# Attention layers: probabilities times V moved behind the scores and transposes of its step; semaphores cleared by ranges

## The reference, cut to what matters

```
# layer 0 (16 heads of 32)
qkv = (xin @ Wqkv.T + qkv_bias) ...; q, k, v = (qkv[0], qkv[1], qkv[2])
qn = q / jnp.maximum(jnp.linalg.norm(q, axis=-1, keepdims=True), 1e-12) * sm
scores = jnp.einsum('bhqd,bhkd->bhqk', qn, kn) + attn_bias
p = jax.nn.softmax(scores, axis=-1)
o = jnp.einsum('bhqk,bhkd->bhqd', p, v)
return o @ Wproj.T + bproj
# layer 1: 16 query heads of 32 on 4 key heads, rotary embedding, a mask that leaves
#          a window of 64 keys, every 64th key and no later block of 128
# layer 2: 8 query heads of 64 on 1 key head, rotary embedding, no mask
# each: scores -> softmax -> times V -> output projection -> added to x
```

## Time and profile before

| | us |
|---|---|
| runs, median (lowest to highest of 3) | 2793.87 (2792.99 to 2800.02) |
| the profiled execution's own time | 2805.94 |
| its span in the profile | 2804.2 |
| PE busy | 2407.7 (86%) |
| DVE busy | 1560.3 (56%) |
| ACT busy | 1279.6 (46%) |
| POOL busy | 902.2 (32%) |

### The profile page before, as it was taken

The page is one execution under the profiler, slowest core; times in us unless marked ns, Lnnn a source line. Parts: engine busy times, 40 slices in busy tenths (PEclk is TensorE's granted clock), DMA queues, the critical chain, the costliest instruction groups (busy, mean ns, idle before and its releaser), DMA issues. The chain is left out here.

```text
span 2804.2 us, 47282 instructions
## 1 busy us (share of the span) xinstructions
PE 2407.7 (86%) x15672; PEld 1952.3 (70%) x15672; DVE 1560.3 (56%) x4470; ACT 1279.6 (46%) x3188; POOL 902.2 (32%) x988
## 2 busy tenths in 40 slices
PE   6888888897699999588788768889899999996776
PEld 4777777786487888466565557777688888885565
DVE  5867767776553434565556466557543333334866
ACT  3666766767321111377665656566531111102443
POOL 0333343423476667123222213223211211211321
PEclk8889999998899999778778679999999999997898
DMA  6000000000110100210000010000100000001000
GB/s 253 1 2 2 9 2 9 2 9 16 61 46 16 44 2 0 74 61 2 2 1 1 1 42 1 1 0 1 46 23 23 23 23 22 0 0 49 8 23 31
DMA packets 17096, 65.29 MB, mean 23 GB/s; under 512 B 3293, under 2 KB 4061, under 8 KB 12277
## 3 DMA queue, kind: packets, MB, share of 16 engines
q1 hardware_dynamic: 16884, 62.70, 6.2%
HBM read 57.42 MB, written 5.28 MB: 22 GB/s over the span
## 5 line engine op out<-in xcount | busy, mean ns | idle before, releaser
L1948 POOL TENSOR_TENSOR l2m_hidl<-l2m_hid,l2m_hidh 128x512 fp32r<-128x512 f32 x64 | 101.0, 1578 | 449.2 <-DVE l2m_hidh L1918 449.2
L1093 ACT ACTIVATE l0a_prob<-l0a_prob,l0a_nmin 128x512 f32<-128x512 f32 x256 | 185.5, 726 | 120.5 <-DVE l0a_nmin L1375 120.0
L1813 ACT ACTIVATE l2m_gate<-l2m_psG 128x512 f32<-128x512 f32 x64 | 38.3, 599 | 437.5 <-PE l2m_psU L1744 436.7
L1570 POOL TENSOR_TENSOR l0a_prob<-l0a_prob,l0a_rinv 128x512 f32<-128x512 f32 x64 | 66.9, 1046 | 483.2 <-DVE l0a_rinv L1382 483.2
L1913 DVE TENSOR_TENSOR l2m_hid<-l2m_gate,l2m_psU 128x512 f32<-128x512 f32 x64 | 44.0, 688 | 282.3 <-ACT l2m_gate L1813 282.3
L1105 ACT ACTIVATE l0a_PT<-l0a_psT 128x512 f32<-128x512 f32 x256 | 152.0, 597 | 55.0 <-PE l0a_psO L946 35.0
L1375 DVE CUSTOM_DVE_ANT_0 l0a_prob<-l0a_psS,l0a_mask 128x512 f32<-128x512 f32 x256 | 175.4, 689 | 1.9 <-PE l0a_psS L904 1.4
L1968 POOL TENSOR_TENSOR res_X<-res_X,l0m_share 128x512 f32<-128x512 f32 x128 | 162.9, 1300 | 24.5 <-DVE l0m_share L1902 23.3
L925 PE MATMUL l0a_psT<-res_ident,l0a_prob 128*128 128x128 f32 x1024 | 165.4, 287 | 3.6 <-ACT l0a_PT L1105 3.3
L780 PE MATMUL l0a_psA<-res_l0a_wh,res_hTh 128*128 128x128 f32 (+1 forms) x512 | 156.0, 305 | 12.7 <-PEq L75 6.7
L1817 ACT ACTIVATE l0m_hid<-l0m_psG,l0m_b1c 128x512 f32<-128x512 f32 x64 | 43.9, 690 | 266.6 <-PE l0m_psG L1744 266.6
(11 more groups left out here) (410 smaller groups left out, 7678.7 us busy)
## 6 DMA issues: line engine op xcount, KB each, us to landing
res_l2m_stage<-in_l2m_w SPq DMA_DIRECT2D x8, 1536.0 KB, 6.5
res_l0m_stage<-in_l0m_w SPq DMA_DIRECT2D x8, 1024.0 KB, 4.8
cond_w<-in_wmod SPq DMA_DIRECT2D x6, 1024.0 KB, 15.8
res_X<-in_x SPq DMA_DIRECT2D x4, 1024.0 KB, 14.2
l1a_wmod<-in_wmod SPq DMA_DIRECT2D x4, 1024.0 KB, 5.8
out<-res_X SPq DMA_DIRECT2D x16, 256.0 KB, 2.0
l_stage<-in_l_w SPq DMA_DIRECT2D x3, 1024.0 KB, 6.9
cond_stage<-in_l0a_w SPq DMA_DIRECT2D x3, 768.0 KB, 13.3
```

Of the source, the lines that this page charges most:

```text
L1093: act.activation(prob[:, n % NP, 0:w], src[:, 0:w], ACT.Exp, bias=nmin[:, n % NP:n % NP + 1], scale=-1.0, accum_out=ssum[:, n % NP:n % NP ...
L1570: op = pool.tensor_tensor(x, x, r.to_broadcast([P, w]), ALU.mult)
L1948: pool.tensor_tensor(hidl[:, s % 2, m, :], hid[:, m, :], f32(hidh[:, s % 2, m, :]), ALU.subtract).then_inc(hl_done, 1)
```

## The change

In `close` the loop over single semaphores becomes a loop over ranges: `runs` puts the scope's semaphore numbers in order and joins those that follow each other. In `batch` of PE the call of `weigh` moves from the head of the step to behind `scores` and `transposes`, still ahead of the jobs. What is computed, the waits that each call holds and the other engines' programs stay as they are.

```diff
+    def runs(self):
+        nums = sorted(s.num for s in self.sems)
+        firsts = [n for n in nums if n - 1 not in nums]
+        return [(n, next(m for m in range(n, nums[-1] + 2) if m not in nums)) for n in firsts]
...
-                for s in self.sems:
-                    sp.sem_clear(s)
+                for first, after in self.runs():
+                    sp.sem_clear(range(first, after))
...
                     for n, todo, _, m in steps(first, more):
-                        if m is not None and m % 4 == CL and not (first and m == CL):
-                            weigh(b, m // 4 - 1, first)
                         if n + AHEAD < NTILE:
                             scores(b, n + AHEAD, first)
                         elif more and n < NTILE:
                             scores(b + 1, n + AHEAD - NTILE, False)
                         if m is not None and m < NTILE:
                             transposes(b, m, first)
+                        if m is not None and m % 4 == CL and not (first and m == CL):
+                            weigh(b, m // 4 - 1, first)
                         for job, i in todo:
                             run(job, i, b, b + 1, b - 1 if n < NTILE else b)
```

## The result

The changed kernel takes 2828.08 us (median of 4, 2822.1 to 2830.6) against 2793.91 for the kernel before beside it (4 runs, 2792.99 to 2800.02): ratio 1.0107, 95% interval 1.0085 to 1.0129. It is slower by some 34 us where 2800 was forecast, and lies outside the range of 2780 to 2815. Its profiled execution took 2829.92 us, with a span of 2828.1. Two executions further down, one each of two kernels, ran at a granted clock of 0.55 and 0.63 and took 3868.63 and 3515.24 us; they count in the medians and not in the ratios. Lines of the new kernel are 7 further down (`weigh` L953, scores L911 and L916, transposes L932, `PT` copy L1112, q copy L1094, `close` L86).

A forecast was written before the change was run, and what follows sets the result against it. PE, busy 86% of the span, was taken to bound the kernel. Clears -11.2, attention 0 +13, attention 1 +3 and attention 2 +1 gave +5.8 us on 2793.87, rounded 2800; range 2780 to 2815.

The forecast's parts named there:

- Clears, -11.2: Closings between stages: a few range clears replace 196 single ones, saving 11.2 us.
- the two bounds: Range clears: first, one lasts as long as a single clear (11.2 us saved); second, time grows with length (nothing saved).
- rival 1: ACT's queue carries every delay: attention 0 +22, attention 1 +6, attention 2 +3; 2814 us, slower, chance 0.35.
- s = 15, 10.5: Attention 0, last step of a head group: late `PT` copy delays the next job, 0.7 us 15 times, 10.5.
- s = 11 and s = 3, 3.6 and 3.5: Attention 0: late `PT` copy costs 0.4 us 9 times at s = 11, 0.5 us 7 times at s = 3.
- s = 7: Attention 0: projections cover the late copy, and surrounding waits hide any new PE wait for a minimum; 0 us.
- The 4.6 us given back: Attention 0: earlier transposes shorten DVE's waits, so the 17.6 us of terms is lowered to +13.
- DVE's waits to fall below 56.0: Sign in attention 0: DVE's waits for transposes, 56.0 us before, become shorter.
- Attention 1, +3: ACT's 20 waits for `weigh` at 0.4 us, up to +8, against DVE's earlier scores, up to -5; taken +3.
- Attention 2, +1: Earlier scores could win up to 15 us, ACT's 14 waits for `weigh` could cost 14; taken +1.
- Rival 3: Early scores help: attention 2 -10, attention 1 -3, clears -11.2, attention 0 +5; 2775 us, faster, chance 0.07.
- PE's busy time stays within the clock's doing: Sign for the whole kernel: PE's busy time changes only as the clock makes it; no term was charged.

The follow-up runs named there:

- S W T: Clears by ranges and `weigh` moved between the scores and the transposes of its step, against the kernel before: 2809.6 us, ratio 1.0032.
- ranges alone: Clears by ranges, with `weigh` left at the head of the step, against the kernel before: 2790.13 us, ratio 0.9968.

## Why the prediction was wrong, point by point

The order was to cost 13 + 3 + 1 = 17 us and costs 39. The failed steps are the terms of attention 0 that were put at nothing or given back, the count of waits in attention 1 and 2, and the clock left out of the sum.

- **Clears, -11.2.** Right: 11.5 us between the stages, 9 by the times. Of the two bounds it is the first, nearly: the time does grow with the range, but by 1.6 ns a semaphore instead of 53. A second range came in two of the seven closings, attention 2's (59 and 61 ns) and MLP 2's (38 and 42). That PE, DVE and ACT start right behind a closing holds for the first of the three in five closings before, 0.29 to 0.31 us behind the last clear; behind MLP 0's the first, DVE, starts after 4.8 us, and behind the last nothing follows.
- **Where the cost arises: ACT's `PT` copy behind `weigh`.** Right as a mechanism (this was also rival 1's place, whose attention 0, +22, came closest; its +6 and +3 for the other two are half of what was measured). A slot that removes the wait brings attention 1 to 473.8 against 473.9, and with it the order costs 11 us instead of 39.
- **s = 15, 10.5.** Right: 10 to 12, and the timeline shows the 0.7 to 0.9 us at ACT's and PE's waits. By the profiles it is the largest term of the full change: from the minimum of s = 0 to that of s = 4, summed over the 16 head groups, it takes 167.9 and 170.9 us with attention 0 changed and 170.6 with s = 15 alone, against 151.7 to 155.1 in four profiles with the old order.
- **s = 11 and s = 3, 3.6 and 3.5.** About 2 and 1, too high if anything.
- **s = 7, "the waits around it hide that. 0."** This step failed in attention 0: about 15 us alone. The sentence before it named the event ("PE may now wait for a minimum that `weigh` used to cover"); it was priced at nothing though nothing in the rows hides it. The 1.42 us are small; dear is a low level that goes on through projections (0.42 us instead of 0.27 for a matmul above). The earlier trace rows showed `weigh` at 1.94 us at this very s = 7. How much of the full change it makes is less clear: from the minimum of s = 8 to that of s = 12, summed over the head groups, it takes 192.0 us with s = 7 alone moved, but 180.8 and 181.9 in the two profiles with all of attention 0 changed, against a mean of 177.5 (172.2 to 184.5) in seven with `weigh` ahead at s = 7.
- **The 4.6 us given back, and DVE's waits to fall below 56.0.** Wrong: they rose to 64.7, and attention 0 grew by 24 us, more than the 17.6 of its terms before anything was given back. The minimum that comes early is followed by one that waits longer (2.58 us).
- **Attention 1, +3; measured +14.** The term "20 waits at 0.4 would be +8, less DVE's 5" failed in its count: the waits became 34 and 42.9 us, 17 more than before and not 8; the new ones, it seems, are copies that used to arrive behind `weigh`'s end. Of DVE's waits for scores (13.4 us) only 0.9 us were won. PE stood 2.4 us more; its matmuls took 11.5 us longer (3.3 and 9.9 by the means over all profiles).
- **Attention 2, +1; measured +6.** Here too the waits rose in number (14 to 25) and the gain from early scores was not there: S W T, which has early scores, took 411.4 us, not less than 409.1. Rival 3, attention 2 at -10, is refuted.
- **Clock, left out of the sum.** This is the largest error of size: 23 of the 44 us by which the three stages grew are matmuls running longer (20 of 42 by the means). "PE's busy time stays within the clock's doing" hid the very term, and PE's idle time was not, as the prediction began, all that another order could move. The trace of before had the price of the low level: `weigh` takes 1.94 us in the earlier trace rows, at a granted clock of 0.5, and 1.08 in the earlier trace rows, at 1.0. The traces have more long stretches of the low level with the scores ahead (13 of 24 places against 10 of 48); they do not show that a wait of 1.42 us is what prolongs one.
- **The frame.** I took the sum from the median of 2793.87 and held ±0.3% to be the noise; the kernel before has since had medians of 2796.82 to 2803.35, but the ratio stands.

What stays open: the four places summed are 30 us by themselves, all of attention 0 moved gave 23 by time and 24 to 28 in the profile, and in the changed kernel's own profile only one batch has the long stretch of the low level behind s = 7 (17.0 us for the four steps; the others 13.1 to 13.6). The terms may overlap, though 30 and 23 also meet within their uncertainty, and how often that stretch comes in the full change is not known from two executions. Why the low level lasts long in one batch and short in the next, with the same order, is open too.

## What to carry to other kernels

Before moving work back in an in-order queue, find who waits for it on another engine and what stands behind that waiter; here a single-buffered copy at the head of ACT's queue carried some 28 of 39 us. Count the waits that will be new, not only those in the list: a producer that now ends behind its consumer's arrival adds waits where there were none (46 here). And look at the granted clock of the dense work behind a new wait of the matmul engine, not only at the wait's own length: compare busy time at equal instruction counts, over several profiles.

## What the runs showed of the hardware

- A range clear took longer with its range, but little: 32 ns for 3 semaphores, 65 for 25, 79 for 28, 92 for 39 and 100 for 45, or 1.6 ns a semaphore. Single clears took 25 to 39 ns each and came one per 53 ns by the two closings of the earlier trace rows; in the records 175 of 189 start 55 to 59 ns behind the one before.
- The same program has, at the same place, either a short stretch of the low level, granted clock 0.5, (3.4 or 6.8 us) or a long one (13.7 or 20.5); between 3.4 and 20.5 lie 6 us of time (11.7 and 17.5 for the same four steps of ranges alone). The kernel before had two long ones in attention 0 in one profiled execution (batches 0 and 3) and one in another (batch 3). Executions of one kernel scatter by more than one such stretch (2778 to 2798 for ranges alone); that the stretches are the reason is not shown.
- A stage whose order was not touched (attention 1) read 477.1 to 482.4 us in eight profiles, five of them behind a changed attention 0. A difference of 5 us in one stage of one execution says nothing.
